# One graph-transformer layer on one core: keys' rows spread among the projections, the mixer's products in halves, edge windows in two loads, the last digits in one go

## The chip, the core and the metric

One core of a Trainium2 chip runs the whole program. Its engines are named as in the profile: PE (TensorE), DVE (VectorE), ACT (ScalarE), POOL (GpSimd) and SP (SyncE, here only an issuer of DMAs). The metric is device microseconds of one execution, the median of several.

## The reference, cut to what matters

1250 nodes with 512 features, 41250 edges sorted by destination, 8 heads of 64.

```python
xn = layernorm(x)
# graph attention over the edges, on layernorm(xn)*g + b
q, k, v = three projections of it
ws = (q[origin] * k[destination]).sum(-1) * SCALE * edge_weights
values = segment_sum(segment_softmax(ws, origin) * v[destination], origin)
gnn = xn + (values @ W1 + b1) @ W2 + b2
# linear attention ("mixer") over all nodes, on xn
q, k = elu(xn @ Wq + bq) + 1, elu(xn @ Wk + bk) + 1;  v = xn @ Wv + bv
kv = einsum('bshd,bshe->bhde', k, v);  z = 1 / einsum('bshd,bhd->bsh', q, k.sum(axis=1))
mix = einsum('bshd,bhde,bsh->bshe', q, kv, z) @ Wp + bp
x = xn + gnn + mix
# y = layernorm(x); three one-hot digits in columns 64:112 of y are read, shifted, and
# twice a one-hot of the two result digits is added to columns 128:160
out = x + ffn(y)
```

## The kernel before, in words

Every engine has its own instruction stream, written out by hand; they meet only at semaphores, and each stream runs in program order. So a wait holds back all that stands behind it on its engine.

**The edge table.** The attention is done densely: a table `w_tab` in DRAM has one cell of 8 weights for each pair (origin, destination). SP first stores an "empty" marker over it, 22 stretches of columns (`empty(k)`, the first 85 columns, the others 57, 1280 rows of 32 bytes per column), and POOL then scatters the edges' weights into it in 22 chunks of 15 indirect DMAs (L591). The cell numbers of a chunk come from DVE (`detect(k)`, which finds edges that occur twice in a window of 65 edges before each edge). For that, SP loads overlapping windows of `src` and `dst` (L489, L490, L494; 125 partitions, 21 chunks, 80 integers each, so 2625 rows of 320 bytes for each of the two arrays), and DVE converts them (`edges`, L1332). Before any scatter SP issues, in this order: Wk, all the windows, then weights and empties of chunks 0 to 2, then the edges' weights once more for a check (`wchk`, 1.32 MB, 10.5 KB for each of 125 partitions, L519), then chunk 3 and on.

**The projections.** The rows are 10 tiles of 128, in pieces of 4, 4 and 2 tiles (`PIECES`). For each piece PE computes q (4 groups), k (4 groups), v (one group per tile); a group is 4 products in float32, 8 instructions. Each group has a number in the list `PROJ`; group r goes to PSUM bank 2 + r % 4 and must wait until group r-4 was taken out (`proj`, `taken`). ACT takes q, DVE takes k and v. After each piece PE turns the k of the piece (`k_rows`, L1026), ACT copies each turned tile and stores it and the tile of v in `kv_rows` (L727); the copy of tile t waits for the store of tile t-2, and ACT goes on only when DVE has taken v. The bias row of v needs the product of the layer norm's bias with Wv (`fold_row`, L1005 on PE and L1415 on DVE), without which DVE can take no v.

**DVE's order** in this stage is a list of calls (L1442 to L1473): `edges`, `detect(0)`, `detect(1)`, `order_checks`, the four `take_k(0, m)` with detections between, `moments(2)`, `take_x(1)` (the input of piece 1), `fold_row`, `marker_check` (L1354, needs `wchk`), and then `take_v` with a detection after each. Then comes a chain of small instructions that lists the repeated edges and ends in a flag.

**The mixer.** For each tile PE makes mk and mv, and adds kᵀv to two banks (`kv_sum`, L1073: for each pair of heads one 128 by 130 product, of which only the two diagonal halves are used). Then, with W1, W2 and Wp folded together, come the denominators (`den`, L1119), copied by ACT, turned by 20 small products (`zt`, L1137), inverted by DVE (L1586), spread by ACT over 512 columns (`copy_z`), turned again by PE (`zs`, L1149) and multiplied into q by DVE (`scale_q`, L1594), tile by tile; each is followed by the group `my` (L1023).

**The attention** is 30 rounds (3 groups of columns by 10 row tiles) of scores, masks, exponentials, transposes and values. It isn't touched.

**The end.** The last layer norm and the digits are done in two batches, tiles 0 to 7 and tiles 8 and 9 (`FIN`). POOL normalises the first batch (L671), ACT the second (L899). DVE's order is `bits(0)`, `added(28)`, `digits(0)`, `finish(0)`, `added(29)`, `centred(1)`, `gains(1)`, `bits(1)`, `digits(1)`, `finish(1)`; `added(w)` takes PE's last product of the round (L1285). After each `finish`, SP stores that batch whole.

## Time and profile before

| | |
|---|---|
| median of 3 executions | 764.87 us (764.03 to 768.25) |
| the profiled execution's own time | 766.31 us |
| its span, from first to last instruction | 764.6 us |
| busy: PE, DVE, POOL, ACT | 92%, 72%, 53%, 52% |
| mean granted clock of TensorE | 0.98 |

The profile is one execution. Its span leaves out 1.7 us that lie around it, and its own time is 1.4 us above the median, so differences are worked out within the span and then put on the median. "Busy" says nothing of which engine sets the end; for that there are the chain that ended last and each engine's timeline with what ended its idle time.

### The profile page before, as it was taken

Reading aid. Unit: us, or ns where it says so; the run is one execution under the profiler, and the core shown is the slowest. Engines: PE = TensorE matmul, PEld = TensorE weight load, DVE = VectorE, ACT = ScalarE, POOL = GpSimd, SP = SyncE. Lnnn points to the kernel's source line nnn. Section 1 sums busy time; section 2 is a strip of 40 time slices with the busy share of each in tenths; the row PEclk is TensorE's granted clock in tenths of the full one; section 3 lists DMA queues with packets and bytes.
Section 4 is the critical chain, followed back from the end, with each engine's and each line's share of the span. In section 5 each row is a group of like instructions: output and inputs, shape, how many; then the busy total and the mean of one; then the engine's idle time right before and its main releaser. Section 6 shows DMA issues by size and latency. Waiting matters only on the chain.

```text
span 764.6 us, 14029 instructions
## 1 busy us (share of the span) xinstructions
PE 702.1 (92%) x4646; PEld 448.0 (59%) x4646; DVE 552.3 (72%) x1305; ACT 396.1 (52%) x940; POOL 403.2 (53%) x399
## 2 busy tenths in 40 slices
PE   0998599798999999997999999999999999999992
PEld 0544244644444655443666666677777788787870
DVE  4559749395422235235998888899999999999997
ACT  0411220111231213312898989888989987676760
POOL 1007778777777777777777777787710010010011
PEclk9999799999999999999999999999999999999997
DMA  7789795869847398500636354536372434253203
GB/s 239 181 271 357 280 339 199 301 216 367 276 141 244 129 319 299 224 4 4 217 123 224 125 214 135 204 113 223 112 268 112 146 126 164 98 187 104 96 2 134
DMA packets 69638, 143.67 MB, mean 188 GB/s; under 512 B 22187, under 2 KB 54251, under 8 KB 65599
## 3 DMA queue, kind: packets, MB, share of 16 engines
q1 hardware_dynamic: 47084, 119.42, 43.6%
q10 hardware_dynamic: 9136, 17.39, 6.8%
q0 software_dynamic: 13344, 5.92, 3.9%
q8 instruction: 40, 0.66, 0.3%
q14 instruction: 34, 0.28, 0.1%
HBM read 77.99 MB, written 64.80 MB: 187 GB/s over the span
## 4 chain that ended last, share of the span: by engine, by line
PE 75%; DVE 7%; SPq 6%; DMA 5%; issue 4%; ACT 1%; ACTq 0%; DVEq 0%; POOLq 0%
PE bank L1023 16%; PE bank L1221 12%; PE bank L1261 11%; PE bank L1242 10%; PE bank L1017 9%; SPq L490 5%; PE bank L1285 4%; PE bank L1233 3%; DMA V<-in_edge_attr_dram 3%; DVE AR L1687 2%; PE bank L1130 2%; PE bank L1267 2%; DMA kv_rows<-AR 1%; PE bank L1081 1%; PE bank L1226 1%
## 5 line engine op out<-in xcount | busy, mean ns | idle before, releaser
L591 POOL DMA_INDIRECT w_tab<-pay,idx x330 | 341.9, 1036 | 154.2 <-issue 99.4
L852 ACT ACTIVATE AR<-AR,nmx 128x512 f32<-128x512 f32 (+1 forms) x180 | 118.5, 662 | 21.9 <-DVE nmx L1696 21.9
L1687 DVE CUSTOM_DVE_ANT_0 AR<-bank,AR,MX 128x512 f32<-128x512 f32 (+1 forms) x120 | 115.2, 986 | 9.4 <-PE bank L1233 8.1
L1017 PE MATMUL bank<-AR 128*128 128x512 f32 (+1 forms) x288 | 108.0, 535 | 5.5 <-ACT QT L724 3.6
L1221 PE MATMUL bank<-KT,QT 64*128 64x512 f32 (+1 forms) x480 | 105.6, 540 | 6.0 <-ACT bank L860 2.7
L1023 PE MATMUL bank<-AR 128*128 128x512 f32 x240 | 106.9, 600 | 2.5 <-ACT AR L780 2.5
L1261 PE MATMUL bank<-AR,V 128*64 128x128 f32 x1520 | 103.9, 276 | 0.0
L868 ACT ACTIVATE AR<-bank 128x512 f32<-128x512 f32 (+1 forms) x150 | 81.0, 562 | 23.2 <-PE bank L1242 22.7
L1261 PEld LDWEIGHTS bank<-AR,V 128*64 128x64 f32 x1520 | 86.7, 137 | 10.2 <-issue 10.2
L666 POOL DMA_INDIRECT AR<-kv_rows,xd x10 | 10.6, 1062 | 149.1 <-PE bank L1261 132.1
L1017 PEld LDWEIGHTS bank<-AR 128*128 128x128 f32 x288 | 55.9, 197 | 52.9 <-issue 46.0
L1242 PE MATMUL bank<-ident,AR 128*128 128x128 f32 (+2 forms) x660 | 82.8, 273 | 0.5 <-DVE MX L1687 0.3
L1023 PEld LDWEIGHTS bank<-AR 128*128 128x128 f32 x240 | 45.6, 193 | 56.3 <-issue 52.8
L1242 PEld LDWEIGHTS bank<-ident,AR 128*128 128x128 f32 (+2 forms) x660 | 73.9, 139 | 3.0 <-issue 1.6
L860 ACT ACTIVATE bank<-AR 128x512 f32<-128x512 bf16 (+1 forms) x125 | 65.2, 541 | 13.3 <-DVE MX L1687 10.7
L1687 DVE CUSTOM_DVE_ANT_0 AR<-bank,AR 128x512 f32<-128x512 f32 x60 | 63.7, 1088 | 11.4 <-PE bank L1233 11.4
L1221 PEld LDWEIGHTS bank<-KT,QT 64*128 64x128 f32 x480 | 40.2, 185 | 38.6 <-issue 22.2
L1704 DVE COPY AR<-bank 128x512 f32<-128x512 f32 (+1 forms) x70 | 43.4, 644 | 0.3 <-issue 0.3
L852 ACT ACTIVATE bias_row<-bias_row,nmx 128x512 f32<-128x512 f32 (+1 forms) x60 | 39.8, 669 | 3.9 <-DVE nmx L1696 3.9
L733 ACT ACTIVATE AR<-bank 128x512 f32<-128x512 f32 (+1 forms) x10 | 5.9, 595 | 65.1 <-PE bank L1031 41.3
L1687 DVE CUSTOM_DVE_ANT_0 bias_row<-bank,AR,MX 128x512 f32<-128x512 f32 (+1 forms) x40 | 38.1, 991 | 1.8 <-PE bank L1226 1.2
L1023 PE MATMUL bank<-AR,QMN 128*128 128x512 f32 x80 | 35.9, 593 | 0.6 <-DVE QMN L1594 0.6
(270 smaller groups left out, 965.4 us busy)
## 6 DMA issues: line engine op xcount, KB each, us to landing
w_tab<-ztile SPq DMA_DIRECT2D x20, 2280.0 KB, 15.2
AR<-w_tab SPq DMA_DIRECT2D x20, 2048.0 KB
AR<-w_tab SPq DMA_DIRECT2D x10, 1344.0 KB
w_tab<-ztile SPq DMA_DIRECT2D x3, 1800.0 KB, 13.3
w_tab<-pay,idx POOLq DMA_INDIRECT x330
w_tab<-ztile SPq DMA_DIRECT2D x2, 1700.0 KB, 8.9
kv_rows<-AR ACTq DMA_DIRECT2D x9, 256.0 KB, 6.3
kv_rows<-V ACTq DMA_DIRECT2D x9, 256.0 KB
```

The costliest lines, as they stand in the source:

```text
L490: sp.dma_start(to[5:QL, 0, :], view(a, 5 * CJ - HALO, ((CJ, QL - 5), (1, WIN)))).then_inc(s_edges, 16)
L591: pool.indirect_dma_start(out=w_tab, out_offset=bass.IndirectOffsetOnAxis(ap=idx[:, k, j:j + 1], axis=0), in_=pay[:, k % RING, j, :], in_o ...
L852: act.activation(ws[g][u % 4][hh][:, 0:n], ws[g][u % 4][hh][:, 0:n], ACT.Exp, bias=nmx[:, u % 4, hh:hh + 1], accum_out=DG[g][:, c, 2 * p + ...
L860: act.activation(use(("s", u, hh))[:, 0:n], pen[w % 2][:, 0:n], ACT.Copy).then_inc(s_laid, 1)
L868: act.activation(PT[g][u % 4][hh][:, 0:nb * P], use(("t", u, hh))[:, 0:nb * P], ACT.Copy).then_inc(read(("t", u, hh)), 1)
L1017: last = mm(b[:, 0:n], w[:, k, m * P:(m + 1) * P], src_t(k), start=(k == 0), stop=(k == KC - 1))
L1023: last = mm(b[:, :], src_t(k), w[:, k, :], start=(k == 0), stop=(k == KC - 1))
L1221: last = mm(bs[hh][:, 0:m], qs[hh], KT[64 * hh:64 * hh + 64, p, d0:d0 + m], start=not over[hh], stop=over[hh] and g < 2, skip_group_check= ...
L1242: last = mm(use(("t", u, hh))[0:rws, i * P:(i + 1) * P], ws[g][u % 4][hh][:, a:a + rws], ident[:, :], start=(i == 0), stop=(i == len(bl) - ...
L1261: last = mm(bank[7][64 * hh:64 * hh + 64, p * P:(p + 1) * P], v, PT[g][u % 4][hh][0:rws, i * P:(i + 1) * P], start=(i == 0), stop=(i == le ...
L1687: v.tensor_tensor_reduce(out=ws[g][u % 4][hh][:, 0:n], in0=use(("s", u, hh))[:, 0:n], in1=Wt[w % 2][:, 0:n, h], scale=1.0, scalar=MX[g - 1 ...
L1704: v.tensor_copy(PT[g][u % 4][1][:, 0:nb * P], use(("t", u, 1))[:, 0:nb * P]).then_inc(read(("t", u, 1)), 1)
```

## The change

1. **Edge windows in two parts.** The ten one-row loads and the rest of chunk 0 come first, then chunks 1 to 5, then weights and empties of chunks 0 and 1, then the windows of chunks 6 to 21, then `wchk` (now into the free end of QT, in two DMAs), then chunk 2 and on. DVE converts in two parts; the order checks read the integers themselves.
2. **K rows spread.** `k_rows(t)` no longer follows its piece: each tile is turned behind one projection group (`K_BEHIND`), on PE and on ACT.
3. **The bias product of v** is four narrow products side by side (`parts`), then a copy by DVE, then one product that sums them (`fold_row_sum`), which stands on PE between v(0) and v(1). DVE's copy stands in `fold_row`, now behind `marker_check`, `moments(2)` and `take_x(1)`.
4. **The mixer's products.** `kv_sum` from tile 1 on makes only the diagonal halves, 64 by 65, two side by side. The denominators stay turned as they are: DVE inverts them, 512 columns at a time, and PE spreads them with 32-row products side by side in four banks; `zt`, `copy_z` and the 10 `zs` are gone.
5. **Digits once** for all ten tiles, behind `added(29)` and `bits(1)`; **sides stored early**: columns 0 to 127 and 160 to 511 of tiles 0 to 7 are stored as soon as POOL has normalised 4 tiles, the middle 32 columns after the digits.

```diff
+FIRST = 6
+K_BEHIND = {("q", 1, 1): 0, ("q", 1, 3): 1, ("k", 1, 1): 2, ("k", 1, 3): 3, ("v", 5): 4, ("v", 7): 5,
+            ("q", 2, 3): 6, ("k", 2, 3): 7, ("v", 9): 8, ("mq", 0, 1): 9}
+TAU = [("x", 0, k) for k in range(KC)] + [("x", 1, k) for k in range(KC)] + [("k", 0), ("k", 1)]
+TAU += [("x", 2, k) for k in range(KC)] + [("k", t) for t in range(2, NT)]
...
-PROJ += [("w12", 0), ("w12", 1), ("zt",), ("w12", 2), ("w12", 3)] + [("kvw", k) for k in range(KC)]
+PROJ += [("w12", m) for m in range(KC)] + [("kvw", k) for k in range(KC)] + [("my", t) for t in range(NT)]
...
+            def load_windows(i, k0, k1):
                 for a, to in ((src, sW), (dst, dW)):
+                    sp.dma_start(to[:, k0:k1, :], view(a, CE * k0 - HALO, ((CJ, QL), (CE, k1 - k0), (1, WIN)))).then_inc(s_edges[i], 16)
...
-            load_edges()
-            for k in range(3):
+            load_first_chunk()
+            load_windows(0, 1, FIRST)
+            for k in range(2):
                 load_weights_of_edges(k)
                 empty(k)
-            sp.wait_ge(s_idx, 1)
-            sp.dma_start(wchk, w_edge.rearrange("(p t) h -> p t h", p=QL)).then_inc(s_chk, 16)
+            load_windows(1, FIRST, NCH)
+            rows = w_edge.rearrange("(p t) h -> p (t h)", p=QL)
+            sp.dma_start(wchk[:, 0:3, :], rows[:, 0:3 * 704].rearrange("p (m c) -> p m c", m=3)).then_inc(s_chk, 16)
+            sp.dma_start(wchk[:, 3, 0:528], rows[:, 3 * 704:E // QL * H]).then_inc(s_chk, 16)
+            load_weights_of_edges(2)
+            empty(2)
             load_weights_of_edges(3)
...
+            for i in range(2):
+                sp.wait_ge(s_o, 4 * (i + 1))
+                store_sides(4 * i, 4)
+            store_last()
...
             def fold_row():
...
-                for k in range(KC):
-                    last = mm(bank[7][:, :], cols[:, 1, k:k + 1].to_broadcast([P, P]), sWv[:, k, :], start=(k == 0), stop=(k == KC - 1))
-                last.then_inc(s_bp, 1)
+                parts(bank[7], 1, sWv).then_inc(s_bp, 1)
+
+            def fold_row_sum():
+                pe.wait_ge(s_fr, 1)
+                mm(bank[7][:, :], fourth[:, 0:1].to_broadcast([P, P]), folds[0], start=True, stop=True).then_inc(s_bp, 1)
...
                     row_proj("v", t0 + i, sWv, lambda k: x2T[j % 2][:, k, i * P:(i + 1) * P])
-                for m in range(KC):
-                    taken(pe, ("k", j, m))
-                for i in range(n):
-                    k_rows(t0 + i)
+                    if j == 0 and i == 0:
+                        fold_row_sum()
...
+                        for a in range(2):
+                            last = mm(bank[6 + k // 2][64 * a:64 * a + 64, at + HV * a:at + HV * a + HV], KM[t % 2][0:r, k * P + 64 * a:k * P + 64 * a + 64],
+                                      VM[t % 2][0:r, 2 * k + a, :], start=False, stop=(t == NT - 1), skip_group_check=True)
...
+            def spread_z(j):
+                t0, n = PIECES[j]
+                pe.wait_ge(s_z, j + 1)
+                for k in range(KC):
+                    if j:
+                        pe.wait_ge(s_zm, KC * (j - 1) + k + 1)
+                    mm(bank[(0, 1, 6, 7)[k]][:, 0:n * P], pick[32 * k:32 * k + 32, :], zR[32 * k:32 * k + 32, t0 * P:(t0 + n) * P],
+                       start=True, stop=True).then_inc(s_zs, 1)
...
                 last.then_inc(s_pr, 1)
+                if m:
+                    spread_z(m - 1)
...
             def fold_row():
                 dve.wait_ge(s_bp, 4)
+                v.tensor_copy(folds[0], bank[7][:, :]).then_inc(s_fr, 1)
+                dve.wait_ge(s_bp, 5)
                 dve.wait_ge(s_row, 48)
...
-            edges()
+            edges(0, 0, FIRST)
             detect(0)
-            detect(1)
-            order_checks()
             for m in range(KC):
                 take_k(0, m)
-                detect(2 + m)
+            detect(1)
+            edges(1, FIRST, NCH)
+            order_checks()
+            marker_check()
             moments(2)
             take_x(1)
             fold_row()
-            marker_check()
...
+                v.reciprocal(zR[:, t0 * P:(t0 + n) * P], bank[2 + r % 4][:, 0:n * P]).then_inc(s_pf[r % 4], 1)
...
+            for j in range(3):
+                invert_z(j)
+            scale_q(0)
             dve.wait_ge(s_res, NT)
             for t in range(NT):
                 last = v.tensor_tensor(XRES[:, t, :], XRES[:, t, :], bias_row[0][:, :], ALU.add)
+                if t == 4:
+                    scale_q(1)
             ch.link(last)
+            scale_q(2)
...
             bits(0)
             added(NW - 2)
-            digits(0)
-            finish(0)
             added(NW - 1)
             centred(1)
             gains(1)
             bits(1)
-            digits(1)
-            finish(1)
+            digits()
+            finish()
```

## Rows read from the trace of the kernel before

**Rows 1.** The page, chain of work that ended last, shares of the span by engine

```profile
PE 75%; DVE 7%; SPq 6%; DMA 5%; issue 4%; ACT 1%; ACTq 0%; DVEq 0%; POOLq 0%
```

**Rows 2.** Waits between engines, 0 to 130 us: total us, times, longest

```profile
PE bank L1031 <- ACT AR L733: 10.0, 2, 6.0
```

**Rows 3.** PE's timeline, first stages: start us, us, line, tiles, count [idle before <-releaser]

```profile
56.16 3.60 PE L1009 MATMUL bank<-AR,cols 128*128 128x512 f32 x8
...
86.02 15.38 PE L1017 MATMUL bank<-AR 128*128 128x512 f32 x32
...
130.74 1.04 PE L1031 MATMUL bank<-ident,KT 128*128 128x128 f32 x8
...
134.96 7.07 PE L1017 MATMUL bank<-AR 128*128 128x256 f32 x32
145.61 8.86 PE L1017 MATMUL bank<-AR 128*128 128x256 f32 x32 [3.58 <-ACT QT L724]
...
164.05 13.97 PE L1017 MATMUL bank<-AR 128*128 128x512 f32 x32 [1.84 <-issue]
```

**Rows 4.** DVE's timeline, 68 to 84 us, same columns

```profile
68.38 0.74 DVE L1425 TENSOR_SCALAR KT<-bank,kbias 128x512 f32<-128x512 f32 x1
...
71.71 0.69 DVE L1371 BATCH_NORM_STATS2 stat<-XRES 128x6 f32<-128x512 f32 x1
...
74.90 2.74 DVE L1401 SCALAR_TENSOR_TENSOR AR<-AR,cols,QMN 128x512 f32<-128x512 f32 x4
77.56 0.68 DVE L1418 TENSOR_TENSOR bias_row<-bank,bias_row 128x512 f32<-128x512 f32 x1
82.33 0.46 DVE L1355 TENSOR_SCALAR QMN<-V 125x330 f32<-125x330 f32 x1 [4.10 <-DMA V<-in_edge_attr_dram]
...
83.36 0.69 DVE L1430 TENSOR_TENSOR V<-bank,bias_row 128x512 f32<-128x512 f32 x1
```

**Rows 5.** The chain of waits in order of time: start us, us, what

```profile
45.17 1.67 DMA V<-in_dst_dram
...
58.60 23.64 DMA V<-in_edge_attr_dram
```

**Rows 6.** DMA queues, 15 to 24 us: packets, MB, share of 16 engines

```profile
q1 hardware_dynamic: 1891, 0.60, 27.4%
```

**Rows 7.** Stretches of 5 us: busy us of each engine, clock, DMA share, GB/s

```profile
55.00:60.00 5.00, 5.00 (x13) 2.15 (x12) 4.79 (x9) 0.00 (x0) 1.35 (x2) 1.00 1.05 374
```

**Rows 8.** Groups of instructions, page and by form: busy us, mean ns | idle before

```profile
L733 ACT ACTIVATE AR<-bank 128x512 f32<-128x512 f32 (+1 forms) x10 | 5.9, 595 | 65.1 <-PE bank L1031 41.3
L1081 PE MATMUL bank<-AR 128*128 128x130 f32 x72 | 9.5, 274 | 0.0
L1261 PE MATMUL bank<-AR,V 128*64 128x128 f32 x1520 | 103.9, 276 | 0.0
```

**Rows 9.** PE and DVE timelines, end of the mixer, same columns as rows 3

```profile
292.12 7.03 PE L1130 MATMUL bank<-AR 128*128 128x512 f32 x16
...
301.39 0.66 DVE L1586 RECIPROCAL AR<-bank 128x80 f32<-128x80 f32 x1 [4.31 <-PE bank L1137]
...
344.19 7.03 PE L1023 MATMUL bank<-AR,QMN 128*128 128x512 f32 x16
```

**Rows 10.** PE, DVE and SP timelines of the end, same columns as rows 3

```profile
743.38 7.03 PE L1285 MATMUL bank<-AR 128*128 128x512 f32 x16
...
750.18 0.14 DVE L1787 TENSOR_TENSOR AR<-AR 128x8 f32<-128x8 f32 x1
...
754.11 0.68 DVE L1748 TENSOR_TENSOR XRES<-bank,XRES 128x512 f32<-128x512 f32 x1
...
757.88 0.17 DVE L1787 TENSOR_TENSOR AR<-AR 128x2 f32<-128x2 f32 x1
...
761.23 0.40 SPq L546 DMA_DIRECT2D out_dram<-XRES  x1
```

**Rows 11.** The page, DMA queue of POOL: packets, MB, share of 16 engines

```profile
q0 software_dynamic: 13344, 5.92, 3.9%
```

More of the change, by code:

```diff
@@ L261, in gps_layer @@
         ksE = ar(17408, KC * 32).rearrange("p (k h) -> p k h", k=KC)
-        dT = ar(17952, NP)
-        zN = ar(21032, NT * H).rearrange("p (t h) -> p t h", t=NT)
-        zb = [ar(19520 + 512 * i, 512) for i in range(2)]
+        zR = ar(17952, NP)
+        pick = ar(19520, P)
         iota_i = ar(20544, 330).bitcast(I32)
@@ L337, in gps_layer @@
         s_pad = sem("pads_ready")
-        s_edges = sem("edges_loaded")
+        s_edges = [sem(f"edges_loaded{i}") for i in range(2)]
         s_x = [sem(f"x_loaded{j}") for j in range(3)]
@@ L556, in _ @@
                 load_tile(w)
[L557 to L559 removed]
+            for i in range(2):
+                sp.wait_ge(s_o, 4 * (i + 1))
+                store_sides(4 * i, 4)
+            store_last()
+            sp.wait_ge(s_out, 16 * 7)
         @block.gpsimd
@@ L723, in take_q @@
                         act.wait_ge(s_be, 1)
+                    if j == 1 and m == 0:
+                        act.wait_ge(s_ck, 1)
                     act.activation(QT[:, m, t0 * P:(t0 + n) * P], bank[2 + r % 4][:, 0:n * P], ACT.Identity,
                                    bias=qbias[:, m:m + 1], scale=SCALE).then_inc(s_pf[r % 4], 1)
+                    if ("q", j, m) in K_BEHIND:
+                        k_rows(K_BEHIND["q", j, m])
             def k_rows(t):
@@ L759, in _ @@
                     residual(j + 1)
-                t0, n = PIECES[j]
-                for t in range(t0, t0 + n):
+                for t in ((), (2, 3, 4, 5), (7, 8))[j]:
                     k_rows(t)
@@ L807, in _ @@
                 act.activation(W1T[:, m, :], bank[2 + r % 4][:, :], ACT.Copy).then_inc(s_pf[r % 4], 1)
-            for j, (t0, n) in enumerate(PIECES):
-                r = PROJ_OF["den", j]
-                act.wait_ge(s_pr, r + 1)
-                act.activation(dT[:, t0 * P:(t0 + n) * P], bank[2 + r % 4][:, 0:n * P], ACT.Copy).then_inc(s_pf[r % 4], 1)
             r = PROJ_OF["kvt",]
@@ L826, in _ @@
                     act.activation(to[:, m, :], bank[2 + r % 4][:, :], ACT.Copy).then_inc(s_pf[r % 4], 1)
-                if what == "w12":
-                    copy_z(0)
-                    copy_z(1)
-            for t in range(2, NT):
-                copy_z(t)
             def general():
@@ L1018, in qk @@
                     last.then_inc(s_pr, 1)
+                    if (what, j, m) in K_BEHIND:
+                        k_rows(K_BEHIND[what, j, m])
             def row_proj(what, t, w, src_t):
@@ L1024, in row_proj @@
                 last.then_inc(s_pr, 1)
+                if (what, t) in K_BEHIND:
+                    k_rows(K_BEHIND[what, t])
             def k_rows(t):
@@ L1029, in k_rows @@
                 take(tau)
+                for m in range(KC):
+                    taken(pe, ("k", t // 4, m))
                 for k in range(KC):
@@ L1131, in _ @@
                 last.then_inc(s_pr, 1)
-                if m == 1:
-                    b = proj(("zt",))
-                    for j in range(3):
-                        taken(pe, ("den", j))
-                    for t in range(NT):
-                        last = mm(b[:, t * H:(t + 1) * H], dT[:, t * P:(t + 1) * P], fourth[:, :], start=True, stop=True)
-                    last.then_inc(s_pr, 1)
+                if m:
+                    spread_z(m - 1)
             pe.wait_ge(s_mp_l, 16)
@@ L1454, in _ @@
             fold_row()
-            marker_check()
-            for t in range(4):
-                take_v(t)
-                if t == 1:
-                    normed(2)
-                detect(6 + t)
-            for m in range(KC):
+            take_v(0)
+            take_v(1)
+            normed(2)
+            detect(2)
+            take_v(2)
+            detect(3)
+            take_v(3)
+            for k in range(4, 10):
+                detect(k)
+            take_k(1, 0)
+            take_x(2)
+            for m in range(1, KC):
                 take_k(1, m)
-                detect(10 + m)
-            take_x(2)
+                detect(9 + m)
             for t in range(4, 8):
                 take_v(t)
-                detect(10 + t)
-            for m in range(KC):
-                take_k(2, m)
-                detect(18 + m)
-            for t in range(8, NT):
-                take_v(t)
+                detect(9 + t)
+            detect(17)
+            detect(18)
+            take_k(2, 0)
+            take_k(2, 1)
+            detect(19)
+            take_k(2, 2)
+            take_k(2, 3)
+            detect(20)
+            take_v(8)
+            detect(21)
+            take_v(9)
             place_checks()
```

164 lines of the change are left out of this document (72 added, 92 removed).

## The prediction

> **What bounds the kernel now.** I read four views in this order. The page's chain gives PE three quarters of the span [rows 1]: PE's program is nearly one long chain, so an edit is worth what it takes out of PE's time or of the idle time between PE's instructions. The waits then say where PE stood in the early stages. In 0 to 130 us the largest avoidable one is the turning of K rows, 10.0 us in two waits for ACT's copy [rows 2]. The timelines of PE, DVE and the chain show what stood behind it: ACT waited for v, DVE took no v before its marker check, and that check waited until 82.3 us for a load issued at 58.6 [rows 4, 5]. So PE's hole before q of piece 1, at 86.0 [rows 3], was a late DMA. The later holes are smaller: K rows of piece 1 from 130.7 to 135.0 for 1.8 us of work, 3.6 us before 145.6, 1.8 us before 164.05 [rows 3]. The clock is read last. The 32 products that begin at 86.02 took 15.4 us, those at 164.05 took 14.0; of the 32 narrower ones those after the 3.6 us hole took 8.9 and those before it 7.1 [rows 3]. A hole costs some 1.5 to 1.8 us more in clock, and the 1.84 us one cost nothing.
>
> The end is DVE's: PE finishes at 743.4 + 7.0 = 750.4 and DVE works on to 761.2 [rows 10].
>
> **K rows, windows and the bias product.** These act on one point, so they are costed together. In the new order PE does k of piece 0 until 56.2 [rows 3], four narrow products (about 1 us), v(0) until about 60.7, and then must wait for DVE's copy in `fold_row`, behind which stand v(1) to v(3) and q of piece 1. DVE reaches that copy only after `edges`, second part, `marker_check`, `moments(2)` and `take_x(1)`. So the question is when the two loads land.
>
> Windows: uncontested, the queue moved 1891 packets in 9 us, 210 per us, while using 27% of 16 engines [rows 6]; a transfer over 125 partitions keeps about five of the sixteen busy. The 5500 window packets are thus 26 us of those five, and with the other loads on them they landed at 46.8 [rows 5]. Now two empties stand ahead of the second part: (85 + 57) columns by 32 bytes by 1280 rows is 5.8 MB, at 374 GB/s [rows 7] 15.5 us, and about 0.5 us for two loads of weights. The ring is served in order, so the second part lands at 46.8 + 16, less about 1 us of one-row loads that are no longer last: 62. The marker's 1.32 MB goes over the same five engines, 5/16 of 374 GB/s, so 11.3 us: 73.5. The same sums give 46.9 + 21.8 (three empties) + 1.5 + 11.3 = 81.5 for before, and it landed at 82.2 [rows 5]; I trust them to 1 or 2 us.
>
> The Trainium skill, "DMA: Bandwidth & Descriptors", section "Why a DMA increments its semaphore by 16 and not by 1", says that the number of engines is the largest divisor up to 16 of the slowest dimension, which is 5 for 125. The share above bears this out for the windows.
>
> DVE: a `take_k` with a detection takes 3.3 us (68.4 to 71.7), the marker check 1.0 (82.3 to 83.4), `moments(2)` 3.2, `take_x(1)` 2.7, the copy 0.7 [rows 4]. It is free at 56.2 + 3.3 = 59.5, waits for the windows until 62, converts them and does the order checks by 66.5 (integers instead of a float copy: nothing, hidden by the next wait), waits for the marker's weights until 73.5, and copies until 81.1. PE's hole is 60.7 to 81.2. Then come the sum (0.9), three v groups (10.4), and 2 us for the clock: q of piece 1 starts at 94.4, where it started at 86.0. That is **8.4 us later**.
>
> From there the spread pays: 2.4 us of the K rows of piece 1, 3.6 and 1.8 of holes, 1.8 and 1.5 of clock, 11.1 in all [rows 3]. Less four K tiles that now stand behind q(1) and k(1) instead of before (1.8), and less new waits of PE for ACT's copies between `k_rows(1)` and the inputs of piece 2; a copy takes 0.6 us [rows 8], two or three of them stand in the way, 1.5 us (0 to 3). Net 7.8. So PE is **0.6 us later** at the mixer than before. The DVE chain that ends in the flag starts after v(9) and waits again for a product behind mq(0); it keeps PE's shift. POOL's scatters start 20 us earlier, but nobody waits for them there.
>
> **kv_sum.** The whole product is 9.5 us / 72 = 132 ns per instruction, 8 of them 1.06. The nearest row with two 64-wide tiles side by side costs 103.9 / 1520 = 68 ns per instruction with 128 columns streamed [rows 8]. The new one has 16 instructions of 65 columns: 0.55 us if the cost follows the columns, 1.09 if each keeps 68 ns. Bounds for nine tiles: 4.6 us gained to 0.3 lost. I take 0.3 each, **2.7 us**, nearer the lower end of cost since side-by-side tiles stream at once. The Trainium skill, "TensorEngine Tiling (Array Packing)", section "Key Properties", says that changing the tiling mode drains the engine; there are two changes per tile here. No row shows that drain alone; were it 0.25 us each, nothing of the gain would be left.
>
> **Denominators.** From 292.1 to 351.2 PE spends 59.1 us [rows 9]. What stays is 15 groups at 3.45, 51.8. Added are three spreads (0.9, 0.9, 0.5). Added too is DVE's inversion: 0.66 us for 80 columns against 0.68 for a sum of 512 [rows 4, 9]. With the 0.16 us that the smallest instructions take [rows 10] it costs 6.2 ns per column, so 3.3 us for 512, and up to 4.2 without that deduction. It starts behind the bias sums, at about 291; w12(0) needs its bank, so it starts at 294.3: 2.2 us of hole (to 3.1). With 0.8 for ACT's last copy and 0.4 of waits between, 57.5: **1.6 us less**. If the 2.2 us hole costs clock as the 3.6 us one did, nothing is gained here; if the inversion were as cheap as a sum, 3.8.
>
> **The end.** `added(29)` can start at 750.5 instead of 754.1: 3.6. The digits and the last sum take 3.9 us for 8 tiles (750.2 to 754.1) and 3.3 for 2 (757.9 to 761.2) [rows 10], so about 4.1 for 10: 0.8 back, and 0.1 elsewhere. 2.7 remain. A third DMA is issued last, 0.4, and the first moves 1024 pieces of 128 bytes, 64 per engine. The nearest small writes cost at most 3.9% of 16 x 764.6 us / 13344 = 36 ns [rows 11], so 2.1 us, of which the 0.4 of issue hide some: 1.4. **0.9 us less**, between 0 and 1.7. The side stores are over by 755.
>
> The Trainium skill, "DMA: Bandwidth & Descriptors", section "Specifications", gives 512 bytes as the least for line rate, with read-modify-write below. If that doubled the pieces' time, the end would gain nothing.
>
> **Sum:** +0.6 - 2.7 - 1.6 - 0.9 = -4.6. The profiled span of 764.6 becomes 760.0, its own time of 766.3 becomes 761.7, and the median of 764.9 becomes **760.3**.
>
> **The rivals.**
> - *The loads are hidden.* If the second windows and the marker's weights land before DVE asks, nothing holds it between 59.5 and the copy: 2.2 + 2.1 + 1.0 + 3.2 + 2.7 + 0.7 puts that at 71.5, 9.6 us earlier, and all behind it shifts: 750.7. For it speaks that the DMAs had pauses before 45 us; against it that the five engines of the windows had none.
> - *The loads come later: slower.* The windows got 5500 packets through in about 44.8 us of real company, 8.1 ns each [rows 5]. If the 4000 of the second part need that behind the empties, 32.6 us instead of 19, the marker lands at 87, PE's hole grows by 13.6, and the time is 773.9. The place is the wait in `marker_check` with `fold_row_sum` behind it on PE; it loses from a landing at 78 on, and measurably from 82. Against it: most of the other loads are over by then.
> - *The small parts give nothing.* Halved products cost the same, and the 2.2 us hole costs clock: 764.6, no change. For it: both rest on rows far away.
> - *The order doesn't bite.* If DVE's wait ends as forecast but PE's new waits for K copies double, 762.
>
> **How the numbers follow.** A measurement here tells 0.5%, 3.8 us, from nothing. Forecast (757.5 to 763) 0.45; loads hidden 0.2; small parts nothing 0.15; more waits 0.05; later loads 0.15. Faster by over 0.5%: 0.2 and some 0.6 of the forecast's 0.45, so 0.47. Slower: 0.15 and 0.02 of accidents. Same: the rest, 0.36. The range takes the hidden loads and stops at 767: above it lies the later loads' case, most of its 0.15.
>
> **What the profile would show.** PE idle from about 60.7 to 81, released by DVE's copy; DVE waiting twice, until 62 and 73.5; q of piece 1 at 94; no hole over 1 us from there to the mixer; kv_sum at 0.75 us; three reciprocals of 3.3 us with w12(0) behind the first; `added(29)` at 750.5 less the shift. The forecast is wrong if the marker's load lands outside 70 to 78, if the reciprocal isn't some 3 us, or if the attention's rounds change.

## The result and the profile after

The changed kernel takes **776.8 us** (median of 4, 774.1 to 778.0), the kernel before on the same chip 766.6: ratio 1.0116, 95% interval 1.0078 to 1.0154. I had forecast 760.3, with a range that took in the hidden loads and stopped at 767. It is slower by 1.2%, and outside the range. Its profiled span is 775.1 us against 764.6, a difference of 10.5, at a granted clock of 0.963 against 0.980.

First the page of the changed kernel, the chain that ended last by engine.

```profile
PE 74%; SPq 7%; DVE 6%; DMA 5%; issue 5%; ACT 1%; another core or an unknown queue 1%; ACTq 0%; DVEq 0%; POOLq 0%
```

It looks like that of before [rows 1]: shares of a chain don't find 10 us. What finds them is PE's timeline, read against the one before at fixed points of the program. The columns are as in [rows 3].

```profile
14.24 0.27 PE L1045 MATMUL bank<-ident,AR 24*128 24x24 f32 x1 [14.24 <-DMA AR<-in_L_gnn_b_dram]
...
58.17 3.70 PE L1028 MATMUL bank<-AR 128*128 128x512 f32 x8
78.79 2.07 PE L1013 MATMUL bank<-AR,fourth 128*128 128x512 f32 x2 [16.92 <-DVE AR L1424]
...
92.13 7.03 PE L1020 MATMUL bank<-AR 128*128 128x512 f32 x16
...
168.35 7.03 PE L1020 MATMUL bank<-AR 128*128 128x512 f32 x16
178.92 0.56 PE L1066 MATMUL bank<-QMN,tri 125*125 125x10 f32 x2 [3.54 <-DMA AR<-in_L_mix_Wv_dram]
...
179.76 9.91 PE L1028 MATMUL bank<-AR 128*128 128x512 f32 x16
...
195.76 8.76 PE L1028 MATMUL bank<-AR 128*128 128x512 f32 x16 [2.25 <-ACT AR L794]
```

Up to 175.4 us, the end of the mixer's first q groups, the change gains: there the kernel before stood at 178.0 (the 13.97 us from 164.05 of [rows 3]), 2.6 us later. Then PE waits for the mixer's Wv, and the groups behind the wait take 9.91 us for 16 products that take 7.03 elsewhere; the granted clock is 0.50 from 178.9 to 185.0 us, half of full speed, and 1.00 before the wait. At the second mk the changed kernel is 4.1 us behind (195.76 against 191.62). So between the two points 6.8 us are lost. What stands in the queues ahead of the mixer's weights is an empty of SP; the changed kernel's row is first, the same chunk's in the kernel before second.

```profile
155.15 0.52 SPq L506 DMA_DIRECT2D w_tab<-ztile  x1
```

```profile
173.01 0.52 SPq L506 DMA_DIRECT2D w_tab<-ztile  x1
```

The next loss stands where the denominators are inverted; DVE's row is first, PE's second.

```profile
295.66 0.69 DVE L1615 TENSOR_TENSOR bias_row<-bias_row 128x512 f32<-128x512 f32 x1 [2.24 <-DMA bias_row<-in_L_mix_bp_dram]
296.39 6.75 DVE L1598 RECIPROCAL AR<-bank 128x512 f32<-128x512 f32 x2
...
299.80 9.64 PE L1152 MATMUL bank<-AR 128*128 128x512 f32 x16 [4.30 <-DVE AR L1598]
...
324.11 34.57 PE L1028 MATMUL bank<-AR,QMN 128*128 128x512 f32 x80 [0.99 <-ACT AR L832]
```

The stage takes 63.4 us, from 295.3 to 358.7, where it took 59.1 [rows 9]: 4.3 lost in place of 1.6 gained. DVE's wait for the bias (`mix_bp`) is new, and it is again SP that came sooner. First the changed kernel's last three empties, and from its chain the bias's load, 7.50 us from issue to landing. Then the kernel before: the bias's load among the DMA issues (KB and us to landing; it was issued at 284.42), and the last three empties.

```profile
273.17 8.89 SPq L506 DMA_DIRECT2D w_tab<-ztile  x3
...
288.07 7.50 DMA bias_row<-in_L_mix_bp_dram
```

```profile
bias_row<-in_L_mix_bp_dram ACTq DMA_DIRECT2D x1, 256.0 KB, 3.2
...
287.68 5.35 SPq L506 DMA_DIRECT2D w_tab<-ztile  x3
```

Before, the empties were issued 3.3 us behind the bias's load, which landed in 3.2 us, before DVE asked for it. Now they stand ahead of it, the DMA engines are busy all the time until 294 us, and it takes 7.5 us; with 3.2 it would have landed at 291.3, before DVE's 293.4. In the five other traces of changed kernels with usual times that I read for it the load takes 6.5 to 8.5 us. No run held these empties back, so this cause is read from traces and not tested.

The third loss is where nothing was changed, at the first scores of the attention. The rows: PE's timeline, then the transfers of the code queue q8 in the stretches 361 to 362 and 364 to 365 us.

```profile
364.03 3.78 PE L1226 MATMUL bank<-KT,QT 64*128 64x512 f32 x8 [5.35 <-issue]
```

```profile
q8 instruction: 1, 0.02, 6.7%
...
q8 instruction: 1, 0.02, 9.2%
```

Before, the same eight products took 1.99 us behind 2.14 us of idle time. DVE's first use of the scores comes 12.7 us later than before (368.40 against 355.70), and from there to the end of PE's last product it is 394.7 us in both. The end gains:

```profile
756.05 7.03 PE L1290 MATMUL bank<-AR 128*128 128x512 f32 x16
...
757.66 4.81 SPq L550 DMA_DIRECT2D out_dram<-XRES  x4
...
770.70 0.49 DVE L1837 TENSOR_TENSOR XRES<-XRES,AR 128x320 f32<-128x320 f32 x1
...
771.22 0.37 SPq L555 DMA_DIRECT2D out_dram<-XRES  x1
771.64 0.58 SPq L556 DMA_DIRECT2D out_dram<-XRES  x1
772.26 0.47 SPq L557 DMA_DIRECT2D out_dram<-XRES  x1
```

From PE's end to the end of the span it is 12.0 us, where it was 14.2 [rows 10]. The account: front 2.6 gained, mixer's weights 6.8 lost, kv_sum and around it 0.9 gained, denominators 4.3 lost, first scores 5.2 lost, end 2.2 gained. Together 10.6 lost, and the spans differ by 10.5.

### The profile page after: what moved, and what is told of

It is laid out like the page before. It is cut to its first block, busy times and chain, and to the rows that moved or that the text cites. A ratio compares the mean times of both kernels' runs of the same rounds, so it can differ in the third digit from the quotient of the medians.

```text
span 775.1 us, 14051 instructions
## 1 busy us (share of the span) xinstructions
PE 698.1 (90%) x4646; PEld 439.4 (57%) x4684; DVE 560.3 (72%) x1298; ACT 389.5 (50%) x927; POOL 395.8 (51%) x399
## 4 chain that ended last, share of the span: by engine, by line
PE 74%; SPq 7%; DVE 6%; DMA 5%; issue 5%; ACT 1%; another core or an unknown queue 1%; ACTq 0%; DVEq 0%; POOLq 0%
PE bank L1028 18%; PE bank L1226 12%; PE bank L1266 11%; PE bank L1247 10%; PE bank L1020 8%; PE bank L1290 4%; SPq L487 4%; PE bank L1238 2%; PE bank L1152 2%; DVE AR L1713 2%; PE bank L1272 2%; DMA AR<-in_L_mix_Wv_dram 2%; DMA QT<-in_edge_attr_dram 2%; SPq L511 1%
## 5 line engine op out<-in xcount | busy, mean ns | idle before, releaser
L602 POOL DMA_INDIRECT w_tab<-pay,idx x330 | 335.4, 1016 | 146.8 <-issue 97.8
L1226 PE MATMUL bank<-KT,QT 64*128 64x512 f32 (+1 forms) x480 | 107.3, 548 | 9.6 <-issue 5.4
L1028 PE MATMUL bank<-AR 128*128 128x512 f32 x240 | 111.9, 621 | 2.3 <-ACT AR L794 2.3
L677 POOL DMA_INDIRECT AR<-kv_rows,xd x10 | 10.6, 1060 | 175.2 <-PE bank L1266 158.0
L869 ACT ACTIVATE AR<-bank 128x512 f32<-128x512 f32 (+1 forms) x150 | 81.0, 562 | 23.5 <-PE bank L1247 23.0
L1713 DVE CUSTOM_DVE_ANT_0 AR<-bank,AR 128x512 f32<-128x512 f32 x60 | 63.8, 1092 | 16.4 <-remote 16.4
L1290 PE MATMUL bank<-AR 128*128 128x512 f32 x80 | 35.8, 592 | 0.0
```

What stands on the lines that cost most here:

```text
L602: pool.indirect_dma_start(out=w_tab, out_offset=bass.IndirectOffsetOnAxis(ap=idx[:, k, j:j + 1], axis=0), in_=pay[:, k % RING, j, :], in_o ...
L869: act.activation(PT[g][u % 4][hh][:, 0:nb * P], use(("t", u, hh))[:, 0:nb * P], ACT.Copy).then_inc(read(("t", u, hh)), 1)
L1028: last = mm(b[:, :], src_t(k), w[:, k, :], start=(k == 0), stop=(k == KC - 1))
L1226: last = mm(bs[hh][:, 0:m], qs[hh], KT[64 * hh:64 * hh + 64, p, d0:d0 + m], start=not over[hh], stop=over[hh] and g < 2, skip_group_check= ...
L1290: last = mm(use(("y", w)), (tb_last if w == NW - 1 else tb)[:, k * P:(k + 1) * P], W12[:, k, :], start=(k == 0), stop=(k == KC - 1))
L1713: v.tensor_tensor_reduce(out=ws[g][u % 4][hh][:, 0:n], in0=use(("s", u, hh))[:, 0:n], in1=Wt[w % 2][:, 0:n, h], scale=1.0, scalar=MX[g - 1 ...
```

## The experiments

The experiments fell on four chips. On two the kernel before takes 767 us. On the other two, called slow chips here, every kernel takes 1084 to 1144, the one before too: up to some 550 us all engines stand idle again and again for what the profile calls issue or an unknown queue, as in the chain of one of them (the kernel with the shorter branch, below). Times from these chips say nothing of a few microseconds; what stands behind 600 us there runs as elsewhere and is used.

```profile
PE 46%; another core or an unknown queue 28%; DVE 12%; issue 10%; ACT 1%; DMA 1%; ACTq 1%; DVEq 0%; POOLq 0%
```

### The first scores: code that is not there

Between mixer and attention all engines read a flag and jump over a branch that handles rare inputs. The queue q8 moves 0.66 MB in 40 transfers, so 16 KB each; PE's program, counted at 64 bytes an instruction, is 40 such blocks of 256. Both lead to one theory: PE's jump lands in a block that isn't loaded. Positions below are in blocks, by my count of the program; a trace shows only the transfers.

**a_code_shifted** moves PE's program by 144 instructions (one instruction holds two of these waits).

```diff
+            for _ in range(288):
+                pe.wait_ge(s_const, 1)
             pe.wait_ge(s_const, 14)
```

> The changed kernel with 144 wait instructions, long satisfied, at the start of PE's stream, where PE idles until 14.2 us anyway; nothing else. Theory (late code): the instruction queue q8 moves 16 KB, 256 instructions, at a time; counted over the program, the changed kernel's skipped branch lies from 8.48 to 10.00 such blocks and jumps just past the second block, so PE waits for code: 5.35 us of idle time before the attention against 2.14 before, and the clock falls. Shifted, the jump goes from 9.04 to 10.56, still within the two blocks, so the idle time falls back to about 2.1 us, no q8 transfer stands ahead of the first scores, and the time is 4 to 5.5 us less than the changed kernel's 776.8, about 772. Rival: the gap comes from the flag, a semaphore or the mask that DVE writes. Then it stays at 5.3 us and the time is unchanged.

**b_jump_longer** lengthens the branch in the kernel before, **a_branch_shorter** shortens it in the changed one; it leaves 24 transposes out of a branch that is not taken.

```diff
                     for k in range(KC):
-                        last = nc.tensor.transpose(...)
+                        for _ in range(15 if c == 0 else 1):
+                            last = nc.tensor.transpose(...)
```

```diff
-                    for k in range(KC):
+                    for k in range(KC if c < 2 else 1):
                         last = nc.tensor.transpose(bank[0][:, k * P:(k + 1) * P], QT[:, k, c * P:(c + 1) * P], ident[:, :])
```

> The kernel before, with 56 more transposes inside the branch that is never taken: no executed instruction is changed. Theory (late code): the jump now goes from 8.17 to 10.12 blocks instead of to 9.68, past the second block, so a q8 transfer stands ahead of the first scores, the idle time before them grows from 2.14 to about 5.3 us, and the kernel is 3 to 5.5 us slower than the kernel before. Rival (the gap of the changed kernel has another cause): no difference.

> The changed kernel with 24 transposes left out of PE's branch that is never taken: what is executed stays instruction for instruction, PE's start too. The shift by wait instructions was a poor test: those waits cost PE 2.9 us at its start and put the jump close to the edge of a block, and its executions fell into two groups, 771 to 772.6 and 775 to 778. Here the jump goes from 8.48 to 9.81 blocks of 256 instructions. Theory (late code): idle time before the attention about 2.1 us in place of 5.35, no clock lost there, time 4 to 5.5 us less than the changed kernel's 776.8, 771 to 773. Rival: the position within a block is not what counts, and the gap stays at 5.3 us.

**a_branch_loop** turns the branch's last ten repetitions, c = 1 to 9, into a loop (`with pe.Fori(1, NT) as c:`); nothing that runs is changed.

> The changed kernel with the never-taken branch of PE shortened by a loop; what is executed is unchanged. From the q8 transfers of the runs so far: they come 0.25 of a block before the counted positions are whole, so some 64 instructions precede those that I count, and two blocks are at hand. Real positions of jump and target: kernel before 8.42 to 9.93 (just inside block 9), changed 8.73 to 10.25 (outside), jump made longer 8.42 to 10.37 (outside), branch shorter by 24 transposes 8.73 to 10.06 (still outside, and it still waited 5.3 us). Here 8.73 to 9.46: inside. Theory: idle time before the attention 2.2 us, spans in one group, time 4 to 5.5 us less than the changed kernel's 776.8. Rival: another cause that both shifted runs hit by luck; then 5.3 us as before.

> The same kernel as a_branch_loop. In all four kernels with the looped branch PE's idle time before the attention was 2.1 to 2.2 us. On a chip at the usual speed: 4 to 5.5 us less than the changed kernel, about 772, ratio 1.004 to 1.008 to the kernel before. Rival: the five microseconds are given back later and it stays at 776.

The first scores in a_code_shifted, b_jump_longer, a_branch_shorter and a_branch_loop_3, from PE's timelines:

```profile
360.55 1.99 PE L1228 MATMUL bank<-KT,QT 64*128 64x512 f32 x8 [2.21 <-issue]
```

```profile
356.91 3.62 PE L1222 MATMUL bank<-KT,QT 64*128 64x512 f32 x8 [5.65 <-issue]
```

```profile
711.16 3.79 PE L1226 MATMUL bank<-KT,QT 64*128 64x512 f32 x8 [5.28 <-issue]
```

```profile
357.93 1.99 PE L1234 MATMUL bank<-KT,QT 64*128 64x512 f32 x8 [2.12 <-issue]
```

| kernel | jump, target | q8 transfer between jump and scores | idle before scores |
|---|---|---|---|
| before | 8.17, 9.68 | none | 2.14 |
| changed | 8.48, 10.00 | yes, 361 | 5.35 |
| b_jump_longer | 8.17, 10.12 | yes, 353 | 5.65 |
| a_branch_shorter | 8.48, 9.81 | yes, 708 | 5.28 |
| a_code_shifted | 9.04, 10.56 | none | 2.21 |
| a_front_early (below) | 9.04, 10.56 | yes, 341 | 5.43 |
| a_kv_full (below) | 8.11, 9.62 | yes, 358 | 4.96 |
| a_branch_loop | 8.48, 9.21 | none | 2.21 |

b_jump_longer changes nothing that is executed and is slower: 772.9 us, ratio 1.0064 (1.0029 to 1.0098), span 769.8 against 764.6. a_branch_loop_3 takes 771.1, ratio 1.0033 (1.0004 to 1.0061), where the changed kernel had 1.0116. a_branch_shorter (1123.2 us, ratio 1.0046) and a_branch_loop (1110.1, ratio 1.0056, 0.987 to 1.025) fell on a slow chip, where the times can't tell. In all nine kernels with the loop the idle time was 2.1 to 2.2 us. Over all twenty traces, the eight with a q8 transfer between jump and scores have 4.96 to 5.75 us of idle time, the twelve without have 2.1 to 2.2. That PE waits there for code is shown from both sides. The clock is a part by itself: four of those twelve lost some too behind their 2.1 us (c_combined_3's eight products took 3.46 us instead of 1.99). The first form of it was not exact: a_branch_shorter, counted to 9.81, still waited. The transfers come at counted positions about a quarter of a block before the whole number, so some 64 instructions stand ahead of those I count. With them the rule that fits is that the jump must land in the block it starts in or the next; the loop's idle time was forecast by it. The Trainium skill, "Runtime: NRT & Kernel Launch", section "Instruction fetch mechanics", says this: blocks of 256 instructions, a window of two, and a stall when a taken branch leaves it. The traces agree, at 3 us of idle time and some 2 of clock per miss, but for the two runs that follow.

One thing stays open. a_front_early has PE's program of a_code_shifted and missed, and a_kv_full missed though its jump should by the count be within two blocks. They had not made the last transfer that was due before the jump (the last at 276 and 294 us), which a_code_shifted had (337). So a jump can also lose to a late transfer; why it was late I don't know. In time a_code_shifted missed its expectation: 775.9 us median (771.3 to 778.2), 0.9 less than the changed kernel and not 4 to 5.5. Its executions scatter as if both happened; the traced one, at 772.1, is among the fast. Its start was also 2.9 us later.

### The front: DVE's copy

**a_front_early**, with the shift of a_code_shifted (and the wait and the copy taken out of `fold_row`):

```diff
                 take_k(0, m)
-            detect(1)
+            dve.wait_ge(s_bp, 4)
+            v.tensor_copy(folds[0], bank[7][:, :]).then_inc(s_fr, 1)
             edges(1, FIRST, NCH)
             order_checks()
-            marker_check()
             moments(2)
             take_x(1)
             fold_row()
             take_v(0)
+            marker_check()
             take_v(1)
+            detect(1)
```

> The changed kernel with the same shift of PE's code, and DVE's order altered in one place: the copy of the bias product of v comes right behind the last take of k of piece 0, and the marker check behind the take of v(0). Theory: DVE's copy at 78.1 us, behind the wait for the marker's load, holds PE from 61.9 to 78.8; with the copy at about 60 PE goes on at once, q of piece 1 starts near 74 to 76 instead of 92.1, and most of that stays: 10 to 18 us less than the shifted kernel. Rival: PE then runs into later waits (copies of K rows, the mixer's weights, whose loads ACT issues behind its own work and which contend with the empties), and only 3 to 8 us of it are left.

753.7 us, ratio 0.9807 (0.9752 to 0.9861), 22 us less than a_code_shifted, more than the 10 to 18 expected. Its PE timeline:

```profile
63.66 1.02 PE L1013 MATMUL bank<-AR,fourth 128*128 128x512 f32 x2
64.52 10.46 PE L1028 MATMUL bank<-AR 128*128 128x512 f32 x24
74.82 7.03 PE L1020 MATMUL bank<-AR 128*128 128x512 f32 x16
...
161.19 0.36 PE L1068 MATMUL bank<-QMN,tri 125*125 125x10 f32 x2 [0.53 <-DMA AR<-in_L_mix_Wv_dram]
```

The hole of 16.9 us is gone, q of piece 1 starts 17.3 us sooner than in the changed kernel, though PE began 2.9 us later because of the 144 instructions. Some of the rest is the wait for Wv, 3.9 us in a_code_shifted and 0.5 here, and the clock behind it. Of the rival, little: at the first scores PE is still 16.4 us ahead. The traced executions differ by 14.5 us only (spans 755.7 and 770.2), because this one paid for late code at the scores and that one didn't; the 22 us are between medians of kernels that scatter by 7 to 9 us.

### The mixer's weights

**a_empties_later_3** is a_branch_loop_3 with this on SP (a_empties_later and a_empties_later_2 are the same edit, on the shorter and the looped branch, on a slow chip; the wait holds SP, so all later chunks wait too):

```diff
                 sp.wait_ge(s_pay[k % 4], 16 * (k // 4))
+                if k == 11:
+                    sp.wait_ge(s_mv_l, 16)
```

> a_branch_shorter with one wait on SP: the weights and empties of chunk 11 and on stand behind the landing of the mixer's Wv. Theory: three transfers that SP issued at 155 to 159 us, 20 us sooner than in the kernel before, shared the queues with the mixer's weights and made Wk and Wv land at 178.8; with them away the weights land about 172 to 175, PE's hole of 3.5 us at 175.3 and the half clock behind it (9.9 us for a group pair of 7.1) go: 4 to 6 us less than a_branch_shorter. Rival: the K and V stores and ACT's own issues set the landing; then nothing.

> a_branch_loop with chunk 11's weights and empty on SP behind the landing of the mixer's Wv. Theory: the transfers issued at 155 to 159 us delay the mixer's weights; without them the hole at 175.3 (3.5 us) and the half clock behind it go: 4 to 6 us less than a_branch_loop. Rival: ACT's issue at 163.6 to 166 is what is late, the landing moves by under 1 us, and so does the time.

> The same kernel as a_empties_later_2. Theory: PE's hole before the mixer's first mk (3.5 us) and the half clock behind it go, 4 to 6 us less than a_branch_loop_3. Rival: the landing of the mixer's weights is set by when ACT issues them and by ACT's own stores; then under 1 us.

765.5 us, ratio 0.9968 (0.9932 to 1.0003), 5.6 less than a_branch_loop_3; on the slow chip 1133.5 and 1114.6, no less than the 1123.2 and 1110.1 of the kernels without the edit, which tells nothing. SP's and ACT's issues in a_branch_loop_3, PE behind them, then ACT and PE in a_empties_later_3:

```profile
154.95 1.45 SPq L511 DMA_DIRECT2D pay<-in_edge_attr_dram  x1
156.45 1.60 SPq L506 DMA_DIRECT2D w_tab<-ztile  x1
...
164.06 1.43 ACTq L780 DMA_DIRECT2D AR<-in_L_mix_Wv_dram  x1
...
167.22 5.26 ACTq L805 DMA_DIRECT2D AR<-in_L_gnn_W_dram  x1
...
177.89 0.36 PE L1066 MATMUL bank<-QMN,tri 125*125 125x10 f32 x2 [3.34 <-DMA AR<-in_L_mix_Wv_dram]
```

```profile
162.40 0.59 ACTq L782 DMA_DIRECT2D AR<-in_L_mix_Wv_dram  x1
...
163.84 0.75 ACTq L807 DMA_DIRECT2D AR<-in_L_gnn_W_dram  x1
...
174.72 0.36 PE L1068 MATMUL bank<-QMN,tri 125*125 125x10 f32 x2 [0.16 <-DVE QMN L1536]
```

Without the two empties, issued at 154.3 and 156.5, the weights land in time, and even ACT's issue of the next load takes 0.75 us in place of 5.26. The theory stands and the rival falls: Wv is issued 1.7 us sooner and is there at least 3.2 us sooner, and the time is 5.6 us less, as expected.

### The denominators

**a_z_first**, **a_z_first_2**: the three `invert_z(j)` ahead of the wait for the bias `mbp` and its sum.

```diff
+            for j in range(3):
+                invert_z(j)
             dve.wait_ge(s_mbp_l, 16)
             ch.link(v.tensor_tensor(bias_row[0][:, :], bias_row[0][:, :], bias_row[1][:, :], ALU.add))
-            for j in range(3):
-                invert_z(j)
```

> a_branch_shorter with one pair of DVE instructions moved: the three inversions of the denominators stand ahead of the wait for the mixer's output bias (the load that landed at 295.6) and of its sum. Theory: that wait held the first inversion for 2.24 + 0.7 us, so the first group with W2 starts about 2.9 us sooner behind the denominators, PE's hole of 4.3 us shrinks to 1.4, and the clock loss (9.64 us for 16 products that take 7.03) goes too: 3 to 5 us less than a_branch_shorter. Rival: the inversion itself (3.4 us) sets the hole; then under 1 us.

> a_branch_loop with the three inversions ahead of the wait for the mixer's output bias. Where that bias had landed in time the hole before the first group with W2 was 2.10 us, and 1.67 with the inversions first; in the changed kernel it was 4.30 with 2.24 us of waiting for the bias. Theory: hole 1.5 to 2 us, clock kept, 3 to 5 us less than a_branch_loop. Rival: the inversion's own 3.4 us is what counts and the hole costs clock at 2 us as well; then 1 us or less.

Both fell on a slow chip (1121.6 and 1093.8 us). There the bias had landed in time, and the edit took the hole from 2.10 us (a_branch_loop) to 1.67, under 1 us: the expectation of 3 to 5 isn't met where the bias is in time. At the usual speed the place shows in a_branch_loop_3 without the edit and in c_combined_3 with it:

```profile
297.31 9.26 PE L1152 MATMUL bank<-AR 128*128 128x512 f32 x16 [4.89 <-DVE AR L1606]
```

```profile
276.22 7.13 PE L1152 MATMUL bank<-AR 128*128 128x512 f32 x16 [1.67 <-DVE AR L1606]
```

3.2 us of hole and 2.1 of clock. How long the hole is doesn't settle the clock: ahead of these same 16 products 2.10 us cost nothing in a_branch_loop and 1.6 in a_empties_later (8.72 us), 3.34 cost 3.0 in a_code_shifted (10.11), and 2.96 cost nothing in a_kv_full:

```profile
299.25 7.13 PE L1148 MATMUL bank<-AR 128*128 128x512 f32 x16 [2.96 <-DVE AR L1594]
```

Since c_combined_3 differs in the front too, this is the stage's part and not a time measured alone.

### kv_sum and the end

**a_kv_full**, **a_kv_full_2**: whole 128 by 130 products for all tiles, as before.

> The changed kernel with the whole 128 by 130 products in kv_sum for all tiles, as before; PE's code is shifted so that the jump stays within two blocks (8.11 to 9.62). Compare with the shifted kernel. Theory from the two traces: a tile (product and the group behind it) takes 7.68 us with halves and 7.76 whole, so the halves bring 0.08 each, 0.7 in all: this one is 0 to 1.5 us slower. Rival (my forecast): the halves bring 0.3 each and this one is 2.7 slower; other rival: mode changes cost more than they bring, and this one is faster.

> a_branch_loop_3 with the whole products in kv_sum. Theory from the traces: 0.08 us a tile, so 0 to 1.5 us slower than a_branch_loop_3's 771.1 (in the trace: product and following group pair 7.76 instead of 7.68). Rival, my forecast: 0.3 a tile, 2.7 slower. Other rival: the changes between whole and half array cost more than the halves save, and it is faster.

One tile in a_kv_full, then one in the changed kernel:

```profile
249.83 7.03 PE L1028 MATMUL bank<-AR 128*128 128x512 f32 x16
256.70 1.06 PE L1090 MATMUL bank<-AR 128*128 128x130 f32 x8
257.59 7.03 PE L1028 MATMUL bank<-AR 128*128 128x512 f32 x16
```

```profile
249.60 7.13 PE L1028 MATMUL bank<-AR 128*128 128x512 f32 x16
256.66 0.69 PE L1094 MATMUL bank<-AR 128*64 128x65 f32 x16
257.28 7.13 PE L1028 MATMUL bank<-AR 128*128 128x512 f32 x16
```

A period is 7.76 us whole and 7.68 in halves. The product shrinks from 0.89 to 0.62, the groups beside it grow from 6.87 to 7.06: 0.08 a tile, 0.7 for nine, shown by the traces. The times can't tell: a_kv_full takes 772.5, 3.4 less than a_code_shifted and not 0 to 1.5 more, but it started 2.6 us sooner (fewer added waits) and both are mixed up with the late code; a_kv_full_2 fell on a slow chip, 1119.2, with no kernel beside it to compare with.

**b_end_only**: the kernel before with the fifth part of the change alone.

> The kernel before with the change's last part alone: digits once for all ten tiles, sides of tiles 0 to 7 stored early. From the two traces: PE's last product to the end of the span took 14.2 us before and 12.05 after, so 2.1 us less than the kernel before, 1.5 to 2.5; my forecast said 0.9 (0 to 1.7). Rival: the difference lay in the landing of the last transfers by chance; then under 1 us. The times alone can't tell 2 us, the stretch from PE's end to the last transfer can.

763.7 us, ratio 0.9955 (0.9926 to 0.9985). PE's last product and SP's last issue:

```profile
744.57 7.03 PE L1291 MATMUL bank<-AR 128*128 128x512 f32 x16
...
760.79 0.47 SPq L552 DMA_DIRECT2D out_dram<-XRES  x1
```

From 751.6 to the end of the span at 763.7 are 12.1 us, 2.1 less than before: as expected. The time fell by 3.6, between 1 and 6 by the interval, which fits.

### All together

**c_combined** to **c_combined_3**: the early copy, the inversions first, and the shorter (c_combined, with chunk 11 later too) or looped branch. **c_combined_4** adds the wait for chunk 11 to c_combined_3.

> All of it together: DVE's copy of the bias product early and the marker check behind v(0), inversions ahead of the bias, chunk 11 behind the mixer's Wv, the shorter branch. If the parts add up: early copy 14 to 18 us, code 5, inversions 3 to 5, empties 0 to 1 here (the copy's move already let the loads land in time: 0.5 us of hole at 160.7): 776.8 less 24 to 28, so 749 to 753 for a plain sum, below both kernels. From the run with the early copy alone (753.7, which still had the gap of 5.4 us and the slow start): 753.7 less 5.2 less 4, 743 to 746. Rival: PE gets ahead of something else (POOL's scatters before the attention, or the loads), and the time stays at 750 or above.

> The changed kernel with DVE's copy of the bias product early, the marker check behind v(0), the inversions first, and the shorter branch. a_front_early gave 753.7 with the gap of 5.4 us and a start 2.9 us late. Less 5.2 for the gap, 3 for the inversions, 1 for the start: 743 to 747, 2.5 to 3% less than the kernel before. Rival: PE now catches up with loads or with POOL and 750 or more is left.

> The same kernel as c_combined_2, on a chip on which the kernel before takes its usual 765 us if it is to be had. Expectation as there: 743 to 747 us, 2.5 to 3% less than the kernel before; rival: 750 or more, because PE catches up with loads or with POOL.

> c_combined_3 with chunk 11's weights and empty behind the landing of the mixer's Wv. If the parts add: 746.0 less the 3.1 us of hole and some 1 to 2 of clock that a_empties_later_3 gained, 741 to 743. Rival: in the earlier order the chunks that SP holds back are others, the weights land as late as before, and it stays at 746.

c_combined_3 takes **746.1 us**, ratio 0.9712 (0.9653 to 0.9771), below both kernels and within 743 to 747. Its clock is 0.988. It still has 3.24 us of wait for Wv. Whether chunk 11's wait takes that out is open: c_combined_4 fell on a slow chip (1124.4, ratio 1.0068), as did c_combined (1134.4, 1.0148) and c_combined_2 (1105.4, 1.0136). There the early copy brings nothing, and the 3% are measured on one chip with usual times only.

## Why the prediction was wrong, step by step

- **Front, forecast +0.6, measured -2.6.** The wait that decides was right, its size 2.3 us off: PE's hole was forecast from 60.7 to 81.2 and was from 61.9 to 78.8, because the marker landed at 70.9 and not at 73.5; q of piece 1 started at 92.1, not 94.4. From there to the mixer PE needed 83.3 us where it had needed 92.0 [rows 3], 8.8 less where I had 7.8; the largest hole was 1.1 us, as good as said. These two make the difference. PE's start 2.7 us sooner (14.24; its first row before stands at 16.91) is no part of it: k of piece 0 ends at 57.2, where it ended at 56.2, because of a hole of 2.2 us that ended at 40.7 and 1.7 of clock behind it. Of DVE's two waits only one came, the windows had landed when it asked:

```profile
60.62 0.28 DVE L1339 CAST oc<-V 125x240 f32<-125x240 int32 x1
...
70.89 0.62 DVE L1360 TENSOR_SCALAR QMN<-QT 125x264 f32<-125x264 f32 x1 [5.81 <-DMA QT<-in_edge_attr_dram]
```

So 5.8 of the hole's 16.9 us were the wait for the marker's load; the rest was DVE's own work ahead of the copy. a_front_early shows that the copy's place behind all of it cost 17 us, which I priced and didn't question.
- **"POOL's scatters start 20 us earlier, but nobody waits for them there."** This step failed. Nobody on PE's path waits for the scatters, but SP does for the ring slots they free. It sent two empties and two loads of weights 18 us sooner, into the window in which ACT loads the mixer's weights: 6.8 us lost, and a_empties_later_3 won 5.6 by holding them back. The last three empties came 15 us sooner as well, ahead of the load of the mixer's output bias: the next item. I had followed the queues up to the marker's load and stopped there.
- **Denominators, forecast -1.6, measured +4.3.** The inversion was right, 3.37 us per 512 columns against 3.3. The hole was to be 2.2, and is 2.1 where the bias has landed. But "it starts behind the bias sums, at about 291" took the sums as work and not as a wait: the bias landed at 295.6, 7.5 us after its issue, where it had taken 3.2. That is 2.2 us more of hole, and at 4.3 the hole costs 2.6 of clock, which the sum put at nothing. The last 1.2 us are groups (0.7) and spreads (0.5) that took a little more than their terms.
- **kv_sum, forecast -2.7, measured -0.7.** The step "0.3 each" looked at the product alone: 0.27 was right for it. 0.2 of it goes back in the groups beside. The Trainium skill's page "TensorEngine Tiling (Array Packing)", section "Key Properties", says a change of mode drains the engine. The trace fits that with 0.2 us for the two changes of a tile, 0.1 each. My line that at 0.25 each nothing would be left was loose: against a gain of 0.3 a tile, 0.15 each is enough.
- **End, forecast -0.9, measured -2.2, and -2.1 alone (b_end_only).** The 1.4 us for 128-byte pieces was mis-sized (and 64 pieces of 36 ns are 2.3 us, not 2.1): from the end of SP's last issue to the end of the span it is 2.4 us after and 2.6 before. The Trainium skill's least size of 512 bytes ("DMA: Bandwidth & Descriptors", "Specifications") didn't show here; those pieces were on their way while two more issues ran, which may be why.
- **"The attention isn't touched."** Its rounds weren't, its start was, 5.2 us: the change made PE's program 80 instructions longer ahead of the jump. No row that I read could price that. By my count the jump of before, with the 64 instructions ahead, ends at 9.93 of its blocks, 0.07 ahead of an edge; 80 instructions are 0.31.
- **The rivals.** The slower one said 773.9, near the time and for the wrong reason: its loads came sooner, not later. No rival had the two mechanisms that decided.

## What to carry to other kernels

An engine set free earlier releases others. Follow its semaphores two steps on, into every queue, and ask what is in flight there. A wait moved behind another wait costs the later landing, so put what nobody needs yet, here a bias, behind what PE waits for. And count the instructions of the busiest engine around a jump: keep what is jumped over short, with a loop if need be.

## What the runs showed of the hardware

- A jump of PE over 1.5 blocks of 256 instructions costs some 3 us more of idle time when a block has to be fetched behind it (5.35 us against 2.14, with half clock on the next eight products, 3.78 us against 1.99); 80 more instructions ahead of it were enough.
- The clock behind a hole isn't settled by its length: 2.10 us cost nothing or 1.6, and 2.96 cost nothing, ahead of the same 16 products.
- Half-array products cost the whole-array ones beside them 0.2 us per pair of changes (6.87 to 7.06).
- 144 wait instructions, all satisfied, held PE until 17.1 us where it had begun at 14.2.
- While SP's large stores fill the queues, one DMA issue on ACT takes 5.3 us instead of 0.8, and a load of 256 KB lands 7.5 us after its issue instead of 3.2.
